# The second set of experts: two blocks of rows share the short part of their down product

## The reference, cut to what matters

```python
# L1 experts: 8 experts, 2 chosen per token, inner width H = 176
x = hidden_states.reshape(-1, 256)                 # 2048 tokens
scores = softmax(x @ gate_w)
topk_w, topk_idx = top_k(scores, 2)
comb = zeros(T, 8).at[arange(T)[:, None], topk_idx].add(topk_w)
g = silu(einsum('td,edh->teh', x, w_gate)) * einsum('td,edh->teh', x, w_up)
routed = einsum('teh,ehd,te->td', g, w_down, comb)
shared = silu(x @ sw_gate) * (x @ sw_up) @ sw_down
out = routed + shared
```

## Time and profile before

| | |
|---|---|
| three runs | 1171.52, 1172.74, 1173.14 us |
| span of the profiled execution | 1171.5 us |
| PE busy in the span | 1066.6 us (91%) |
| DVE / ACT / POOL busy | 956.1 / 892.2 / 702.5 us |
| second experts, first rows turned to the last answer | 1049.4 to 1147.9 us |
| shares of L2599 and L2615 in the chain that ended last | 4% and 3% of the span |

### The profile page before, as it was taken

The page is one execution under the profiler, slowest core; times in us unless marked ns, Lnnn a source line. Parts: engine busy times, 40 slices in busy tenths (PEclk is TensorE's granted clock), DMA queues, the critical chain, the costliest instruction groups (busy, mean ns, idle before and its releaser), DMA issues.

```text
span 1171.5 us, 24138 instructions
## 1 busy us (share of the span) xinstructions
PE 1066.6 (91%) x8396; PEld 608.8 (52%) x8396; DVE 956.1 (82%) x1748; ACT 892.2 (76%) x1546; POOL 702.5 (60%) x626
## 2 busy tenths in 40 slices
PE   8988898889988988898889988999999999999995
PEld 5743444444444444444444447756654455557774
DVE  6999999999999999999999996853328888843335
ACT  4779999999999999999999996635534567734440
POOL 3016888888787878787878785457641001543331
PEclk9999999999999999999999999799999999999998
DMA  6797987888788888888776664867937003433326
GB/s 192 121 163 146 171 171 162 171 171 173 161 171 171 173 164 173 173 169 164 155 118 110 112 109 65 244 182 213 316 98 300 1 0 85 138 102 101 102 89 222
DMA packets 388928, 176.36 MB, mean 151 GB/s; under 512 B 330542, under 2 KB 373779, under 8 KB 388809
## 3 DMA queue, kind: packets, MB, share of 16 engines
q1 hardware_dynamic: 382104, 157.85, 62.2%
q0 software_dynamic: 6480, 16.77, 4.2%
q10 hardware_dynamic: 224, 0.20, 0.1%
HBM read 52.70 MB, written 43.59 MB: 82 GB/s over the span
## 4 chain that ended last, share of the span: by engine, by line
PE 51%; DVE 33%; ACT 5%; issue 5%; DMA 3%; POOL 2%; SPq 1%; POOLq 0%; ACTq 0%; DVEq 0%
DVE top L426 26%; PE bank L234 10%; PE bank L220 9%; PE bank L1187 4%; PE bank L2599 4%; PE bank L252 4%; PE bank L1580 3%; PE bank L2615 3%; PE bank L1174 2%; PE bank L1166 2%; ACT weight L485 2%; PE bank L270 1%; PE bank L1598 1%; PE bank L682 1%; POOL dispatched_rows L1823 1%
## 5 line engine op out<-in xcount | busy, mean ns | idle before, releaser
L485 ACT ACTIVATE weight<-bank,bias,sq_all 128x1024 uint8<-128x1024 f32 x512 | 610.2, 1201 | 24.1 <-PE bank L234 18.9
L426 DVE TENSOR_REDUCE top<-bank 128x1 f32<-128x512 f32 (+1 forms) x683 | 610.1, 951 | 11.9 <-PE bank L220 1.6
L537 POOL CAST weight<-turned 128x2048 bf16<-128x2048 uint8 x256 | 479.4, 1895 | 44.8 <-PE bank L252 23.2
L234 PE MATMUL bank<-kT,query 128*128 128x512 bf16 x1024 | 307.7, 382 | 11.8 <-ACT weight L485 4.8
L252 PEld LDWEIGHTS bank<-v_sb,weight 128*128 128x128 bf16 x4096 | 172.0, 97 | 103.4 <-POOL weight L537 1.9
L220 PE MATMUL bank<-kT,qspace 64*128 64x512 bf16 x687 | 134.9, 386 | 55.0 <-DVE top L426 55.0
L252 PE MATMUL bank<-v_sb,weight 128*128 128x16 bf16 x4096 | 172.5, 170 | 0.6 <-POOL weight L537 0.6
L220 PE MATMUL bank<-kT,query 128*128 128x512 bf16 x337 | 127.8, 379 | 1.6 <-DVE top L426 1.4
L234 PEld LDWEIGHTS bank<-kT,query 128*128 128x128 bf16 x1024 | 59.8, 96 | 103.8 <-ACT weight L485 61.8
L1823 POOL DMA_INDIRECT dispatched_rows<-qspace,put x32 | 37.1, 1161 | 117.8 <-DVE qspace L2376 108.6
L485 ACT ACTIVATION_READ_ACCUMULATOR weight<-bank,bias,sq_all 128x1 f32 x512 | 101.3, 198 | 0.0
(11 more groups left out here) (350 smaller groups left out, 1466.2 us busy)
## 6 DMA issues: line engine op xcount, KB each, us to landing
dispatched_rows<-zeros SPq DMA_DIRECT2D x32, 524.0 KB, 3.2
answered_rows<-zeros SPq DMA_DIRECT2D x16, 512.0 KB, 3.2
late<-answered_rows SPq DMA_DIRECT2D x16, 512.0 KB, 6.3
erow<-dispatched_rows SPq DMA_DIRECT2D x39, 131.0 KB, 2.1
wgu<-in_L_ffn_w_gate SPq DMA_DIRECT2D x26, 176.0 KB, 3.9
wgu<-in_L_ffn_w_up SPq DMA_DIRECT2D x26, 176.0 KB, 3.9
query<-qspace SPq DMA_DIRECT2D x32, 128.0 KB, 3.1
turned<-weight SPq DMA_TRANSPOSE x256, 3.1
```

The costliest lines, as they stand in the source:

```text
L234: mm = pe.matmul(unit[u % 2][:, v * 512:(v + 1) * 512], query2[:, t % 2, h, :], kT[:, h // 2, first + v * 512:first + (v + 1) * 512], star ...
L426: ve.tensor_reduce(top[:, first:first + count], bank[:, first % 3:first % 3 + count, :], AX.X, ALU.max).then_inc(s_max, 1)
L485: ac.activation(weight8[:, n % BYTES, u * 1024:(u + 1) * 1024], unit[u], ACT.Exp, bias=bias[:, n:n + 1], scale=sq_all[:, n:n + 1], accum_o ...
L537: po.tensor_copy(weight[:, n % 3, :, :, :].rearrange("p c q two -> p (c q two)"), turned8[:, n % 3, :, :].rearrange("p c q -> p (c q)").bi ...
```

## The change

Down weights. Before, all 8 experts' `w_down` lay in `w1d` on 88 partitions, in two pieces. Now `w1d` holds inner rows 0 to 127 of each expert on 128 partitions. A second area, `w1d_rest`, holds the other 48 rows: on partitions 0 to 47 those of all 8 experts (one more transfer in the earlier stage, for the even block of a pair), and on partitions 64 to 111 a ring of 7 places, into which SP fetches the 48 rows of the odd block's owner during the stage (`fetch_rest`, one transfer per pair, after the fetch of the odd block's rows).

Order. Blocks go in pairs j = (2j, 2j + 1); the last pair has one block. PE turns rows two blocks ahead instead of one. In round j it does both hidden products of pair j, then the three transposes of pair j - 1 (128 rows of the even block, the two short pieces side by side, 128 rows of the odd block), then the answers of pair j - 2: two full products over 128 rows, and two short ones over 48 rows on opposite halves of the rows. DVE multiplies each block in two instructions (128 and 48 columns) and copies 384 columns per pair. ACT and DVE follow the same pairs. POOL's loop is as before.

The diff, cut to its core (line numbers of the changed file differ by 2 to 20):

```diff
@@ -1724,7 +1724,8 @@
...
-                w1d = sw[0:FC, 0:E1 * 2 * C].rearrange("p (e c n) -> p e c n", e=E1, c=2)
+                w1d = sw[:, 0:E1 * C].rearrange("p (e n) -> p e n", e=E1)
+                w1d_rest = sw[:, E1 * C:2 * E1 * C].rearrange("p (e n) -> p e n", e=E1)
@@ -1785,7 +1786,8 @@
...
                         for e in range(E1):
-                            sp.dma_start(w1d[:, e, :, :], a["L1_ffn_w_down"][e].rearrange("(c p) n -> p c n", p=FC)).then_inc(s_w1, 16)
+                            sp.dma_start(w1d[:, e, :], a["L1_ffn_w_down"][e, 0:P, :]).then_inc(s_w1, 16)
+                        sp.dma_start(w1d_rest[rest_rows(0), :, :], a["L1_ffn_w_down"][:, P:F1, :].rearrange("e p n -> p e n")).then_inc(s_w1, 16)
@@ -2538,7 +2540,8 @@
...
-                    esil1, eh1, ehT1 = se("esil1", [P, 2, F1]), se("eh1", [P, 2, F1]), se("ehT1", [FC, 2, 2, P])
+                    NPAIR1 = (NB1 + 1) // 2
+                    esil1, eh1, ehT1 = se("esil1", [P, 2, F1]), se("eh1", [P, 2, 3 * P]), se("ehT1", [P, 2, 3, P])
@@ -2549,6 +2552,15 @@
...
+                    RESTS = SLOTS - RING1
+
+                    def rest_loaded(j):
+                        s = RING1 + j % RESTS
+                        return s_ew[s], weights_loaded(s, len(range(s, E0, SLOTS))) + 16 * (j // RESTS + 1)
+
+                    def pair_blocks(j):
+                        return range(2 * j, min(2 * j + 2, NB1))
@@ -2562,12 +2574,20 @@
...
+                        def fetch_rest(j):
+                            if j >= RESTS:
+                                sp.wait_ge(sx_["answers"], E0 + 2 * (j - RESTS) + 2)
+                            e = sp.value_load(owner_u[0:1, 2 * j + 1:2 * j + 2], min_val=0, max_val=E1 - 1)
+                            sp.dma_start(w1d_rest[rest_rows(1), j % RESTS, :], a["L1_ffn_w_down"][e, P:F1, :]).then_inc(rest_loaded(j)[0], 16)
...
                         for b in range(NB1):
                             fetch_rows(b)
+                            if b % 2 == 1:
+                                fetch_rest(b // 2)
@@ -2599,43 +2619,50 @@
...
+                        def turn_hidden(j):
+                            both = len(pair_blocks(j))
+                            pe.wait_ge(sx_["hidden"], E0 + 2 * j + both)
...
+                            for k in range(both + 1):
+                                mm = pe.transpose(bank[:, 4 + j % 2, k * P:(k + 1) * P], eh1[:, j % 2, k * P:(k + 1) * P], ident[:])
                             mm.then_inc(sx_["hidden_turned"], 1)
...
-                        def answer(b):
...
-                            for c in range(2):
-                                mm = pe.matmul(bank[:, 6 + b % 2, 0:C], ehT1[:, b % 2, c, :], w1d[:, expert[b], c, :], start=c == 0, stop=c == 1)
...
+                        def answer(j):
+                            pe.wait_ge(sx_["hidden_copied"], E0 // 2 + j + 1)
+                            for i, b in enumerate(pair_blocks(j)):
+                                if b >= 2:
+                                    pe.wait_ge(sx_["answers_weighted"], E0 + b - 1)
+                                pe.matmul(bank[:, 6 + i, 0:C], ehT1[:, j % 2, 2 * i, :], w1d[:, expert[b], :], start=True, stop=False)
+                            for i, b in enumerate(pair_blocks(j)):
+                                if i == 1:
+                                    pe.wait_ge(*rest_loaded(j))
+                                pe.matmul(bank[:, 6 + i, 0:C], ehT1[rest_rows(i), j % 2, 1, :],
+                                          w1d_rest[rest_rows(i), expert[b] if i == 0 else j % RESTS, :], start=False, stop=True).then_inc(sx_["answers"], 1)
+                                expert.pop(b)
...
                         turn_rows(0)
...
+                        load_owner(1)
+                        turn_rows(1)
+                        for j in range(NPAIR1 + 2):
+                            for b in pair_blocks(j) if j < NPAIR1 else ():
+                                if b + 2 < NB1:
+                                    load_owner(b + 2)
+                                    turn_rows(b + 2)
                                 hidden(b)
...
+                            if 0 <= j - 1 < NPAIR1:
+                                turn_hidden(j - 1)
+                            if j >= 2:
+                                answer(j - 2)
@@ -2666,13 +2693,14 @@
...
+                        copy_rows(1)
+                        for j in range(NPAIR1 + 2):
+                            for b in pair_blocks(j) if j < NPAIR1 else ():
                                 silu(b)
-                            if b >= 2:
-                                weigh(b - 2)
+                                if b + 2 < NB1:
+                                    copy_rows(b + 2)
+                            for b in pair_blocks(j - 2) if j >= 2 else ():
+                                weigh(b)
@@ -2692,25 +2720,35 @@
...
                         def multiply(b):
...
-                            ve.tensor_tensor(eh1[:, b % 2, :], esil1[:, b % 2, :], bank[:, 2 + b % 2, F1:2 * F1], ALU.mult).then_inc(sx_["hidden"], 1)
...
+                            j = b // 2
+                            if j >= 2:
+                                ve.wait_ge(sx_["hidden_turned"], E0 // 2 + j - 1)
+                            main, rest = 2 * P * (b % 2), P + KB * (b % 2)
+                            ve.tensor_tensor(eh1[:, j % 2, main:main + P], esil1[:, b % 2, 0:P], bank[:, 2 + b % 2, F1:F1 + P], ALU.mult)
+                            ve.tensor_tensor(eh1[:, j % 2, rest:rest + F1 - P], esil1[:, b % 2, P:], bank[:, 2 + b % 2, F1 + P:2 * F1],
+                                             ALU.mult).then_inc(sx_["hidden"], 1)
...
+                        def copy_hidden(j):
...
+                            if j >= 2:
+                                ve.wait_ge(sx_["answers"], E0 + 2 * j - 2)
+                            width = P * (both + 1)
+                            ve.tensor_copy(ehT1[:, j % 2, :, :].rearrange("p c n -> p (c n)")[:, 0:width], bank[:, 4 + j % 2, 0:width]).then_inc(sx_["hidden_copied"], 1)
...
+                        for j in range(NPAIR1 + 1):
+                            for b in pair_blocks(j) if j < NPAIR1 else ():
                                 read_payload(b)
                                 multiply(b)
...
+                                if b % 2 == 0:
+                                    sum_payload(b)
+                                    aim(b)
+                            if j >= 1:
+                                copy_hidden(j - 1)
+                            if j < NPAIR1 and len(pair_blocks(j)) == 2:
+                                sum_payload(2 * j + 1)
+                                aim(2 * j + 1)
```

More of the change, by code:

```diff
@@ L2610, in answer @@
-                        def answer(b):
-                            pe.wait_ge(sx_["hidden_copied"], E0 // 2 + b + 1)
-                            if b >= 2:
-                                pe.wait_ge(sx_["answers_weighted"], E0 + b - 1)
-                            for c in range(2):
-                                mm = pe.matmul(bank[:, 6 + b % 2, 0:C], ehT1[:, b % 2, c, :], w1d[:, expert[b], c, :], start=c == 0, stop=c == 1)
-                            mm.then_inc(sx_["answers"], 1)
-                            expert.pop(b)
+                        def turn_hidden(j):
+                            both = len(pair_blocks(j))
+                            pe.wait_ge(sx_["hidden"], E0 + 2 * j + both)
+                            if j >= 2:
+                                pe.wait_ge(sx_["hidden_copied"], E0 // 2 + j - 1)
+                            for k in range(both + 1):
+                                mm = pe.transpose(bank[:, 4 + j % 2, k * P:(k + 1) * P], eh1[:, j % 2, k * P:(k + 1) * P], ident[:])
+                            mm.then_inc(sx_["hidden_turned"], 1)
@@ L2619, in experts1_tensor @@
                         expert = {}
[L2620 removed]
+                        pe.wait_ge(s_w1, 16 * (3 * E1 + 1))
                         pe.wait_ge(mx_["tables_ready"], 1)
@@ L2705, in experts1_vector @@
-                        for b in range(NB1 + 1):
-                            if b < NB1:
+                            j = b // 2
[5 more added lines that the diff above has]
+                                             ALU.mult).then_inc(sx_["hidden"], 1)
@@ new lines, in copy_hidden @@
+                        def copy_hidden(j):
+                            both = len(pair_blocks(j))
+                            ve.wait_ge(sx_["hidden_turned"], E0 // 2 + j + 1)
+                            if j >= 2:
+                                ve.wait_ge(sx_["answers"], E0 + 2 * j - 2)
+                            width = P * (both + 1)
+                            ve.tensor_copy(ehT1[:, j % 2, :, :].rearrange("p c n -> p (c n)")[:, 0:width], bank[:, 4 + j % 2, 0:width]).then_inc(sx_["hidden_copied"], 1)
```

34 lines of the change are left out of this document (2 added, 32 removed).

## The result

| | before | changed |
|---|---|---|
| median of 12 runs each | 1172.58 us | 1175.53 us |
| lowest to highest | 1170.83 to 1174.66 | 1171.99 to 1177.34 |
| ratio of the times, 95% interval | | 1.0026 (1.0017 to 1.0036) |
| span of the profiled execution | 1171.5 us | 1173.0 us |
| first turning of rows to the final sums, in the profile | 1157.80 - 1049.37 = 108.43 | 1159.05 - 1049.42 = 109.63 |

The changed kernel is slower by 2.95 us by the medians, 0.26% by the ratio. The forecast was 1173.3, +0.6 us, inside a range of 1170.4 to 1176.5. The profiled execution of the changed kernel took 1174.71 us, 1.7 us more than its span and 0.8 us less than the median of its runs. So the two profiles, one execution each, differ by 1.5 us where the medians differ by 2.95; the ratios are the safer measure of what a change costs, and the traces show where.

The account below looks back on a forecast made before the run. TensorE's work bounds the middle; the later of TensorE's path and the last scatter decides. -3.9 + 2.8 + 1.3 = +0.2 us on TensorE's path, +0.6 on the scatter path, so 1172.7 + 0.6 = 1173.3 us, range 1170.4 to 1176.5.

Parts of the forecast that it names:

- Term 1, the middle: TensorE's work in the middle of the second experts: 4.785 us a pair instead of 4.98, -3.9 us in all.
- VectorE's second product: Extra multiply per block on VectorE, put at 0.2 to 0.34 us, costed at nothing because VectorE idles.
- Term 2, the wait at the start: Start of the stage: TensorE waits for block 2's rows and later ones, +2.8 us, bounds 0.9 to 3.8.
- The two smaller waits for rows: Start of the stage: TensorE waits 0.53 us for block 4's rows and 0.26 us for block 6's.
- The last rival: Start of the stage: the matmul clock falls in the 2 us gap; no size given, chance 0.02.
- Term 3, the end: End of the stage: two answer-only rounds make TensorE wait for `weigh`, +1.3 us, bounds 0.9 to 1.6.
- The scatter path: End of the stage: five scatters in line, 1.28 us each, the last at 1150.26, moving the end by +0.6 us.
- Short products in series: Answers in each pair: short products don't run beside each other, 6.3 us more, 1179.6 us; chance 0.08.
- A sequencer that runs late: TensorE's queue: owner loads and waits show as 0.1 to 0.4 us a pair, 1175 to 1180 us; chance 0.10.
- The full gain: Costs at the ends vanish: 1170.5 us without the start's, 1168.8 without either end's; chance 0.12.
- Within 0.2%: Whole kernel: time between 1170.4 and 1175.1 us, not told from no change; chance 0.69.
- "slower": Whole kernel: time over 1175.1 us; chance 0.18.

Follow-up runs that it names:

- e8: Changed kernel with both short products of a pair on the same half of the rows; 1181.9 us, one run.
- e3: Changed kernel with three extra matmuls, results unused, filling the gap before block 2's rows; 1173.53 us, ratio 1.0008 to the kernel before.
- e5: Changed kernel with rows turned one block ahead as before and short weights fetched two pairs later; 1170.71 us, ratio 0.9980 to the kernel before.
- e2: Changed kernel with each transfer of 48 weight rows issued two pairs later in SyncE's queue; 1172.94 us, ratio 1.0000 to the kernel before.

## Why the prediction was right, and where it was wrong

- **Term 1, the middle, -3.9 us: right.** The period is 4.784 us against 4.785 forecast, joint by joint. Reading it off the same form in the first experts was what made this exact; the 0.63 us of the short products was neither the 0.43 of perfect overlap nor the 1.06 that e8 shows without it. The joints' price stood; whether it is the drain of the rule cited beside it was not tried. VectorE's second product took 0.20 us and moved nothing, as was assumed.
- **Term 2, the wait at the start, +2.8 us: right in place and near in size, wrong in what it set off.** The first hidden product came at 1053.10 for 1052.95 forecast. With the clock kept up, the wait costs 2.6 us in the traces and 3.3 by the ratios (e3 against e5). The two smaller waits for rows didn't show in either profile, since the products at half clock took their place.
- **The clock: the step that failed.** The last rival, "The clock falls in the 2 us gap at the start (0.02): rows 1 have 1.00, and the gap is short", was what happened, in both profiles of the changed kernel. The mistake was to read the clock from a dense stretch and to look at the one gap alone. The new gap of 1.83 us stands behind two others, 0.90 and 0.53 us, that were there before the change too, and between them TensorE does 0.4 us of work each. With the tail of the work ahead of them that is 1.37 us of work in 4, for 2.43 before. With the gap filled, the kernel lost 0.9 us to the one before instead of 2.95 (e3). The Trainium skill ("TensorE: Matmul & The Clock Gate", Loop structure matters more than you think) warns that a long wait for a transfer between every matmul lets the engine go cold. These traces agree that waits for transfers do it, and here it did not take one at every matmul: in the changed kernel a wait of 1.83 us behind the two shorter ones was enough.
- **Term 3, the end, +1.3 us on TensorE: too small by 0.4.** From the short products of pair 17 (1143.82) to L1855 (1149.03) it is 5.21 us, not 4.85. Each pause from the short products to the next long one was 1.45 us, not 1.35, and the last block's long product to its short one 0.63, not 0.52. In it the long product comes 0.72 us behind the start of `weigh` (1144.55), not 0.62. A register instruction stands ahead of the product here and not in the first experts; whether that is the cause wasn't tried.
- **The scatter path, +0.6 us: right in form.** Five scatters in line, the first 2.04 us after the short products, the last at +7.15 us (forecast 7.16). The short products themselves came at 1143.82 for 1143.1 forecast, so the path ended 1.3 us late. e3, where the clock doesn't interfere, gives +0.9 us (interval -0.1 to +1.9), which holds the forecast of +0.6, and is too wide to confirm it.
- **The rivals.** Short products in series (0.08) is ruled out by e8. A sequencer that runs late (0.10) is ruled out by the period: 4.784 us with owner loads and waits in the queue. The full gain (0.12) didn't come, but e5, at 1170.71 us, came where that rival puts the time without the start's part, 1170.5.
- **The forecast's time** was 2.2 us too low, about the clock's 2.1 us, which is itself uncertain by 1.5. Here luck helped: 1175.53 lies above the forecast's own bounds (1171.0 to 1174.6, and 0.5 for the median), and inside the range only because that reached up into the price of the sequencer rival, which did not occur. No term of the sum held the clock. "Within 0.2%" had 0.69 and "slower" 0.18; the measured +0.26% lies just over that border, with an interval that reaches from 0.17% to 0.36%.

Open: why the stretch at half clock lasts 3.4 us in one profile of the same kernel and 6.8 us in another, and why it began in one execution of e2 with the shorter gap. No run tried this. How the 3.3 us (ratios) and 2.6 us (traces) for the wait come together stays open as well; the intervals are wide enough for both.

## What to carry to other kernels

Before an order is changed at the start of a stage, add up what the matmul engine does in the whole stretch around it, old gaps included: a wait of about 2 us behind two older short ones cost 2.6 to 3.3 us as waiting and about 2.1 us as clock. A pipeline that looks one more step ahead needs one more transfer before its first product, and whatever else stands in that queue is in front of it; keep the first round shallow and put transfers that are used later behind those used first. Where steps are paired, the last pair hands the next engine its work in a lump: count that engine's queue after the last product, not only the products.

## What the runs showed of the hardware

- Two 48-row, 256-column products in 32 bit floats on opposite halves of the rows take 0.64 us with their joints (changed kernel), and on the same half 1.06 us (e8). One such product over 88 rows takes 0.43 us, half of the 0.87 for two in the kernel before, and that would be the time of a perfect overlap.
- The granted clock fell to 1.2 GHz after 4 us in which TensorE was busy for 1.37 us, and stayed there through 3 to 6 us of dense work (3.4 us in all in one profile, 6.8 in another). In e2 it fell after 4 us with 1.82 us of work, in which the longest wait was 0.89 us.
- 1.8 us of matmuls whose results nobody reads, put into that gap, left the clock at 2.4 GHz in the profile taken and made the kernel faster by about 2 us (ratio 1.0008 for 1.0026), although they computed nothing. They delayed nothing either: TensorE still waited 0.48 us for the rows behind them.
